# A gathered wide-and-deep network on one core: embedding rows and W1 kept on chip, waits and tail rearranged

## The reference

```python
emb = jax.vmap(lambda tab, idx: tab[idx])(tables, cat_features)      # 26 x 512 x 128
emb_btd = jnp.transpose(emb, (1, 0, 2))
wide_num = jax.nn.relu(numerical @ w_wide + b_wide)
linear_output = jnp.sum(emb_btd, axis=1) + wide_num                  # 512 x 128
x = jnp.concatenate([numerical, emb_btd.reshape(512, 26 * 128)], axis=1)
x = jax.nn.relu(x @ W1 + b1)                                         # W1: 3341 x 256
x = jax.nn.relu(x @ W2 + b2)                                         # 256 x 128
return jax.nn.sigmoid(x @ W3 + b3 + linear_output)                   # 512 x 128
```

## Time and profile before

| | |
|---|---|
| median of 3 runs | 145.16 us (144.66 to 145.37) |
| profiled execution, its own time | 145.52 us |
| its span | 143.7 us |
| PE busy, PEld busy | 89.8 us (62%), 46.8 us (33%) |
| DVE, ACT busy | 28.8 us (20%), 20.5 us (14%) |
| POOL busy | 99.2 us (69%) |
| mean granted TensorE clock | 0.877 of full |
| transfers | 10.75 MB, 75 GB/s over the span |

### The profile page before, as it was taken

One profiled execution on the slowest core, in us unless ns is written; L12 is line 12 of the kernel. 1 busy time (PEld: TensorE's weight loads), 2 busy tenths in 40 slices (PEclk: granted clock), 3 DMA queues, 4 the chain that ended last, 5 costly groups with the idle time before them and its releaser, 6 DMA issues.

```text
span 143.7 us, 1247 instructions
## 1 busy us (share of the span) xinstructions
PE 89.8 (62%) x278; PEld 46.8 (33%) x278; DVE 28.8 (20%) x78; ACT 20.5 (14%) x42; POOL 99.2 (69%) x111
## 2 busy tenths in 40 slices
PE   0588298609760793655944925916909809986891
PEld 0326234204320440232513404404404305444780
DVE  1402012203120211221211211302203202122461
ACT  0401011101110110110111101101101101122342
POOL 2677777777777777777777776776777777777400
PEclk9999999996899559995698797796895995999998
DMA  4424553571357347865254283393362481332311
GB/s 96 132 55 51 52 51 100 74 97 48 91 88 83 55 65 87 79 90 92 51 96 89 39 89 92 47 81 110 51 93 76 72 110 55 81 83 55 54 45 37
DMA packets 8901, 10.75 MB, mean 75 GB/s; under 512 B 3018, under 2 KB 7235, under 8 KB 8899
## 3 DMA queue, kind: packets, MB, share of 16 engines
q0 software_dynamic: 3328, 6.82, 36.6%
q1 hardware_dynamic: 4448, 3.67, 8.9%
q10 hardware_dynamic: 1123, 0.23, 0.8%
HBM read 10.45 MB, written 0.26 MB: 75 GB/s over the span
## 4 chain that ended last, share of the span: by engine, by line
DMA 39%; PE 27%; POOL 18%; issue 8%; POOLq 1%; DVE 0%; ACT 0%
DMA emb<-in_L_rec_tables,staged 35%; PE first_layer L232 15%; POOL emb L180 14%; PE turn L225 10%; POOL emb_tail L180 4%; DMA emb_tail<-in_L_rec_tables,row_idx 2%; DMA emb<-in_L_rec_tables,row_idx 2%; POOLq L31 1%; PE first_layer L283 1%; PE mlp L295 1%; PE scalars L305 0%; ACT y L484 0%; DVE h L417 0%; PE turn L273 0%; POOLq L198 0%
## 5 line engine op out<-in xcount | busy, mean ns | idle before, releaser
L180 POOL DMA_INDIRECT emb<-in_L_rec_tables,staged x88 | 83.0, 943 | 27.9 <-issue 22.6
L232 PE MATMUL first_layer<-emb_t,w 128*128 128x512 f32 x96 | 59.4, 753 | 0.4 <-DMA w<-in_L_rec_W 0.4
L225 PE MATMUL turn<-ident,emb 128*128 128x128 f32 x96 | 20.3, 350 | 42.9 <-DMA emb<-in_L_rec_tables,staged 38.8
L225 PEld LDWEIGHTS turn<-ident,emb 128*128 128x128 f32 x96 | 14.1, 176 | 64.7 <-DMA emb<-in_L_rec_tables,staged 56.1
L463 ACT COPY emb_t<-turn 128x512 f32<-128x512 f32 x24 | 14.0, 585 | 107.6 <-PE turn L225 107.6
L232 PEld LDWEIGHTS first_layer<-emb_t,w 128*128 128x128 f32 x96 | 21.5, 248 | 18.0 <-issue 16.9
L377 DVE TENSOR_TENSOR emb_sum<-turn,emb_sum 128x512 f32<-128x512 f32 x23 | 15.9, 692 | 39.2 <-ACT emb_t L463 39.2
L365 DVE COPY staged<-row_idx 128x4 int32 (+1 forms) x22 | 4.5, 209 | 55.5 <-DMA emb<-in_L_rec_tables,staged 55.4
L180 POOL DMA_INDIRECT emb_tail<-in_L_rec_tables,row_idx x8 | 7.5, 944 | 2.4 <-issue 2.4
L180 POOL DMA_INDIRECT emb<-in_L_rec_tables,row_idx x7 | 6.6, 943 | 2.1 <-issue 1.8
L283 PE MATMUL first_layer<-emb_tail_t,w_tail 128*128 128x128 f32 x32 | 4.9, 282 | 0.0
(11 more groups left out here) (37 smaller groups left out, 22.5 us busy)
## 6 DMA issues: line engine op xcount, KB each, us to landing
w<-in_L_rec_W SPq DMA_DIRECT2D x24, 128.0 KB, 3.0
emb<-in_L_rec_tables,staged POOLq DMA_INDIRECT x88, 3.6
w_tail<-in_L_rec_W SPq DMA_DIRECT2D x1, 256.0 KB, 3.2
out<-y SPq DMA_DIRECT2D x4, 64.0 KB, 1.8
w<-in_L_rec_W ACTq DMA_DIRECT2D x1, 128.0 KB
emb_tail<-in_L_rec_tables,row_idx POOLq DMA_INDIRECT x8, 2.9
emb<-in_L_rec_tables,row_idx POOLq DMA_INDIRECT x7, 3.8
cat_sb<-in_r_cat_features ACTq DMA_DIRECT2D x1, 52.0 KB
```

What stands on the lines that cost most here:

```text
L180: nc.gpsimd.indirect_dma_start(tile, None, rows, bass.IndirectOffsetOnAxis(ap=index, axis=0)).then_inc(landed, 16)
L225: mm = nc.tensor.transpose(turn[par][:, chunk(c)], emb[:, par, c, :], ident[:, :])
L232: mm = nc.tensor.matmul(first_layer[k][:, :], w1[:, par, chunk(k)], emb_t[:, par, :], start=False, stop=False, skip_group_check=True)
```

## The change

- All 26 tables' rows and all of W1 have a place of their own on chip. W1 comes in four loads at the start (tables 0-1, 2-7, 8-16, 17-25), and the body's loops are written out.
- POOL waits, before table t's gathers, for the landing of table t - 2 (AHEAD), with a semaphore for each table. `staged` and its copies are gone. The row offsets are added in one instruction for all 104 columns; wrap and clamp are done in another order (clamp to -V..V-1, then wrap), with as many instructions.
- TensorE does a table's first layer right behind ACT's copy of that table. `emb_t` has four slots, `turn` two.
- The wide part and the vectors stand ahead of table 0 in TensorE's list, in banks of their own.
- In the tail, `turn_sum` is a matmul of the chunk's `emb_sum` with the identity into a bank `final`, and layer 3 is added in the same bank, as a matmul of `h2` with W3 spread over 128 columns (`w3_wide`, made once by DVE). The sigmoid takes this bank, with the wide part as its bias; `add_wide` is gone. TensorE's order in the tail is another one (below). DVE still adds each tile behind ACT's copy.

The core of the diff (of `...` stretches, those with names alone and with lines removed are left out):

```diff
-PAIR = 2
+LATE = 2
+SLOTS = 4
+AHEAD = 2
+W1_CUTS = [0, 2, 8, 17, 26]
...
-        staged = sb("staged", [P, PAIR, CH], I32)
-        w1 = sb("w1", [P, PAIR, H1])
-        w1_tail = sb("w1_tail", [P, PAIR, H1])
+        w1 = sb("w1", [P, T, H1])
+        ones = sb("ones", [P, D])
+        w3_wide = sb("w3_wide", [P, D])
-        emb = sb("emb", [P, PAIR, CH, D])
-        emb_t = sb("emb_t", [P, PAIR, B])
-        emb_tail = sb("emb_tail", [P, CH, PAIR, D])
-        emb_tail_t = sb("emb_tail_t", [P, CH, PAIR, P])
+        emb = sb("emb", [P, T, CH, D])
+        emb_t = sb("emb_t", [P, SLOTS, B])
+        late_t = sb("late_t", [P, TILES, P])
-        logit = sb("logit", [P, CH])
...
-            def load_w1(step, par, first=False):
-                if not first:
-                    sp.wait_ge(used[par], step)
-                sp.dma_start(w1[:, par, :], W1[bass.ds(NUM + (step * PAIR + par) * D, D), :]
-                             ).then_inc(w1_loaded[par], 16)
-
-            for par in range(PAIR):
-                load_w1(0, par, first=True)
-            sp.dma_start(w1_tail[:, :, :], W1[NUM + TAIL * PAIR * D:NUM + T * D, :].rearrange("(g d) n -> d g n", d=D)
-                         ).then_inc(w1_tail_loaded, 16)
-            with sp.Fori(1, TAIL) as step:
-                for par in range(PAIR):
-                    load_w1(step, par)
+            for i, loaded in enumerate(w1_loaded):
+                lo, hi = W1_CUTS[i], W1_CUTS[i + 1]
+                sp.dma_start(w1[:, lo:hi, :], W1[NUM + lo * D:NUM + hi * D, :].rearrange("(t d) n -> d t n", d=D)
+                             ).then_inc(loaded, 16)
...
             gp.wait_ge(first_steps, 3)
-            gather(emb[:, 0, 0, :], first_row[:, :], gathered[0])
-            gp.wait_ge(first_rows_ready, 1)
-            for par in range(PAIR):
+            gather(0, 0, first_row[:, :], gathered[0])
+            gp.wait_ge(rows_ready, 1)
+            for t in range(BODY):
+                if t > AHEAD:
+                    gp.wait_ge(gathered[t - AHEAD], WHOLE)
                 for c in range(CH):
-                    if par + c == 0:
-                        continue
-                    gather(emb[:, par, c, :], column(par, c), gathered[par])
-            with gp.Fori(1, TAIL) as step:
-                for par in range(PAIR):
-                    gp.wait_ge(staged_ready[par], step)
-                    gp.wait_ge(turned[par], step)
-                    gp.sem_inc(slot_free, 1)
-                    for c in range(CH):
-                        gather(emb[:, par, c, :], staged[:, par, c:c + 1], gathered[par])
-            gp.wait_ge(rows_ready, 1)
-            for c in range(CH):
-                for g in range(PAIR):
-                    gather(emb_tail[:, c, g, :], column(TAIL * PAIR + g, c), tail_gathered[c * PAIR + g])
+                    if t + c > 0:
+                        gather(t, c, column(t, c), gathered[t])
+            gp.wait_ge(gathered[BODY - AHEAD], WHOLE)
+            for c in range(CH):
+                if c == CH // 2:
+                    gp.wait_ge(gathered[BODY - AHEAD + 1], WHOLE)
+                for g in range(LATE):
+                    gather(BODY + g, c, column(BODY + g, c), late_gathered[c * LATE + g])
...
+            pe.wait_ge(small_loaded, 16 * SMALL)
+            for c in range(CH):
+                mm = nc.tensor.matmul(wide_bank[:, c:c + 1], num_t[:, chunk(c)], w_wide_sb[:, :],
+                                      start=True, stop=True)
+            mm.then_inc(wide_done, 1)
+            nc.tensor.transpose(vec_bank[:, 0:KH + 2], vec_rows[:, :],
+                                ident[0:KH + 2, 0:KH + 2]).then_inc(vecs_turned, 1)
+
+            def turn_table(t):
+                pe.wait_ge(gathered[t], WHOLE)
+                if t >= 2:
+                    pe.wait_ge(added, t - 1)
                 for c in range(CH):
+                    mm = nc.tensor.transpose(turn[t % 2][:, chunk(c)], emb[:, t, c, :], ident[:, :])
+                mm.then_inc(turned, 1)
+
+            def sum_table(t):
+                if t in W1_CUTS:
+                    pe.wait_ge(w1_loaded[W1_CUTS.index(t)], 16)
+                pe.wait_ge(copied, t + 1)
+                for k in range(KH):
+                    mm = nc.tensor.matmul(first_layer[k][:, :], w1[:, t, chunk(k)], emb_t[:, t % SLOTS, :],
+                                          start=False, stop=False, skip_group_check=True)
+                mm.then_inc(used, 1)
+
+            for t in range(BODY):
+                turn_table(t)
+                sum_table(t)
+
+            def turn_tile(n):
+                c, g = divmod(n, LATE)
+                pe.wait_ge(late_gathered[n], 16)
+                if n < 2:
+                    pe.wait_ge(added, BODY - 1 + n)
                 else:
+                    pe.wait_ge(late_added, n - 1)
+                nc.tensor.transpose(turn[n % 2][:, 0:P], emb[:, BODY + g, c, :], ident[:, :]
+                                    ).then_inc(late_turned, 1)
+
+            def sum_tile(n):
+                c, g = divmod(n, LATE)
+                pe.wait_ge(late_copied, n + 1)
                 for k, (done, ready) in enumerate([(h1_low_done, h1_low_ready), (h1_high_done, h1_high_ready)]):
                     if c >= 1 and g == 0:
                         pe.wait_ge(ready, c)
+                    mm = nc.tensor.matmul(first_layer[k][:, chunk(c)], w1[:, BODY + g, chunk(k)], late_t[:, n, :],
+                                          start=False, stop=False, skip_group_check=True)
+                    if g == LATE - 1:
                         mm.then_inc(done, 1)
 
+            def turn_sum(c):
+                pe.wait_ge(late_added, (c + 1) * LATE)
+                if c == 0:
+                    pe.wait_ge(wide_ready, 1)
+                    pe.wait_ge(vecs_ready, 1)
                 if c >= 2:
                     pe.wait_ge(y_ready, c - 1)
+                nc.tensor.matmul(final[c % 2][:, 0:D], emb_sum[:, chunk(c)], ident[:, :],
+                                 start=True, stop=False, skip_group_check=True)
+
+            def layer2(c):
                 for k, ready in enumerate([h1_low_ready, h1_high_ready]):
                     pe.wait_ge(ready, c + 1)
                     mm = nc.tensor.matmul(mlp[c % 2][:, 0:P], w2[:, k, :], h1[:, k, chunk(c)],
...
             def layer3(c):
                 pe.wait_ge(h2_ready, c + 1)
                 if c == 0:
+                    pe.wait_ge(w3_ready, 1)
+                nc.tensor.matmul(final[c % 2][:, 0:D], h2[:, chunk(c)], w3_wide[:, :],
+                                 start=False, stop=True, skip_group_check=True).then_inc(final_done, 1)
+
+            for c in range(CH):
+                n = c * LATE
+                turn_tile(n)
+                if c >= 1:
+                    layer2(c - 1)
+                sum_tile(n)
+                if c >= 1:
+                    turn_sum(c - 1)
+                turn_tile(n + 1)
+                if c >= 1:
+                    layer3(c - 1)
+                sum_tile(n + 1)
+            turn_sum(CH - 1)
+            layer2(CH - 1)
             layer3(CH - 1)
...
+            nc.vector.memset(ones[:, :], 1.0).then_inc(ones_ready, 1)
...
+            nc.vector.tensor_tensor(row_idx[:, :], idx_bank[:, 0:T * CH], base[:, :, :].rearrange("p t c -> p (t c)"),
+                                    ALU.add).then_inc(rows_ready, 1)
...
+            nc.vector.tensor_scalar(w3_wide[:, :], ones[:, :], w3_col, None, ALU.mult).then_inc(w3_ready, 1)
+
+            for t in range(BODY):
+                dve.wait_ge(copied, t + 1)
+                if t == 0:
+                    nc.vector.tensor_copy(emb_sum[:, :], turn[0][:, :]).then_inc(added, 1)
+                else:
+                    dve.wait_ge(added, t)
+                    nc.vector.tensor_tensor(emb_sum[:, :], turn[t % 2][:, :], emb_sum[:, :], ALU.add
+                                            ).then_inc(added, 1)
...
+            def add_tile(n):
+                c = n // LATE
+                dve.wait_ge(late_copied, n + 1)
+                if n == 0:
+                    dve.wait_ge(added, BODY)
+                elif n % LATE > 0:
+                    dve.wait_ge(late_added, n)
+                nc.vector.tensor_tensor(emb_sum[:, chunk(c)], turn[n % 2][:, 0:P], emb_sum[:, chunk(c)], ALU.add
+                                        ).then_inc(late_added, 1)
+
+            for c in range(CH):
+                n = c * LATE
                 if c >= 1:
                     relu_h1_high(c - 1)
+                add_tile(n)
+                if c >= 1:
+                    relu_h2(c - 1)
+                add_tile(n + 1)
             relu_h1_high(CH - 1)
             relu_h2(CH - 1)
...
+            for t in range(BODY):
+                act.wait_ge(turned, t + 1)
+                if t >= SLOTS:
+                    act.wait_ge(used, t - SLOTS + 1)
+                nc.scalar.copy(emb_t[:, t % SLOTS, :], turn[t % 2][:, :]).then_inc(copied, 1)
+
```

(15 more changed lines are left out.)

249 lines of the change are left out of this document (50 added, 199 removed).

## The result

| | before | changed |
|---|---|---|
| median beside each other | 145.27 us (144.66 to 146.06, 18 runs) | 145.78 us (145.27 to 147.75, 18 runs) |
| ratio | | 1.0049, 95% interval 1.0026 to 1.0073 |
| the same kernel on a later occasion (e18_alone) | 145.13 us (17 runs) | 145.79 us (12 runs), ratio 1.0059 (1.0021 to 1.0096) |
| profiled execution, its own time and span | 145.52 / 143.7 us | 147.32 / 145.5 us |

The changed kernel is half a per cent slower; 144.6 was forecast. Its times fall into two groups: of the 30 executions of both occasions 11 lie at 146.79 to 147.75, and all others but one (146.14) at 145.27 to 145.87. The trace of the first occasion is one of the upper group, that of e18_alone (145.87) one of the lower.

What follows compares the result with a forecast made beforehand. POOL's gathers, then the dependent work after the last one, bound the kernel. POOL's -1.09 less 1.28 lost at tile 7, with a shorter tail, gave -0.51: 145.0 profiled, less 0.36 for the median, 144.6 us; range 143.3 to 146.7.

Steps and rivals of the forecast that it cites:

- POOL, -1.09: POOL's four stalls ahead of tables that reuse a slot go, since it waits for landings, not transposes: -1.09 us.
- D: Rival: W1's burst reaches POOL at the wait ahead of table 3 or the indices' landing; 145.1 to 146.1, chance 0.10.
- Where the gain is lost: Tile stage at the end: table 23's 3 us are never caught up, tile 7 turns 1.28 us after landing.
- From one layer 2 to the next: TensorE's tile stage: one chunk's cycle takes 2.58 us, while two tiles are gathered in 2.50.
- From there: Tail from tile 7's turn to the end of the last sigmoid: 3.33 us in place of 3.98.
- The store: The store behind the last sigmoid stays at 2.4 us.
- From the profiled execution to the median, -0.36: Last step: the median lies 0.36 us under the profiled execution, taking 145.0 to 144.6.
- Rival B: TensorE meets the end at half clock at table 23's transposes and sums: +2.2 us, 146.8 in full; chance 0.28.
- The sum's bank: Chunk end: without add_wide and chunk 2's transpose and layer 2 ahead of chunk 3's, the tail takes 3.33 for 3.98.

Runs made afterwards that it cites:

- e18_alone: The changed kernel itself, unchanged, with only the kernel before beside it; 145.79 us, ratio 1.0059 to the kernel before.
- e6_turned: e3_both with POOL waiting again for the transposes of the table two before instead of its landing; 146.22 us, ratio 1.0061 to the kernel before.
- e2_tail: The changed kernel with the old order of the tile stage on TensorE, DVE and ACT, body as changed; 144.44 us, ratio 0.9934 to the kernel before.
- e3_both: The changed kernel with both old orders, in the body and in the tile stage; 144.44 us, ratio 0.9933 to the kernel before.
- e5_warm20: The changed kernel with three dummy matmuls of 512 columns behind table 20's first layer; 145.38 us, ratio 1.0020 to the kernel before.
- e1_body: The changed kernel with the old body order, a table's sum behind the next table's transposes, tile stage as changed; 145.64 us, ratio 1.0013.
- e7_wide: e3_both with the old chunk end: transposed sum in layer 2's bank, layer 3 with one column, add_wide on DVE; 144.14 us, ratio 0.9916.
- e8_order: e3_both with the tile stage's lists for TensorE, DVE and ACT written out in an order found by search; 144.17 us, ratio 0.9930.

## Why the prediction was wrong

- **POOL, -1.09: right in size, its cause not shown.** Its last gather is at 132.78 and 132.60 (forecast 132.90), with no stall. The prediction gave all four stalls to the wait for transposes and put the loop and the staged copies at 0. e6_turned has the old wait in a written-out list and none of the four, so what goes away with the loop may be all of the 0.99. That no landing reaches the wait (D) held, although W1's burst did reach TensorE: the wide part waited for its load until 11.95 and table 0 was turned at 14.18, where it was turned at 10.65 before. The prediction took two or three us; it was 3.5. In e6_turned the same lateness cost POOL 2.6 us, so the new wait earns its place at the start, by a term that the sum did not have. Table 1's rows landed there by 17.95, 5.2 after its last gather at 12.77, some 1 us ahead of the wait for them, which the changed kernel reaches near 18.9. Behind this stands the Trainium skill, "DMA: Bandwidth & Descriptors", section "Queues, rings and completion order", with its turns between queues: the trace agrees, since the gathers beside the burst landed, in the changed kernel the first of them in 6.8 us and none in more.
- **Where the gain is lost: right in kind.** Table 23 stands 3 us ahead of a stage that never catches up, as the prediction said with 1.28 lost; e2_tail and e3_both confirm that it is this order's: there TensorE waits for tiles 3 and 5.
- **The failed step: "From one layer 2 to the next", 2.58 us, and "From there", 3.33.** They measured 2.79 and 3.63. Both steps took every instruction at the length that it has in a row without a wait, 0.61 for four. In the new order the first group behind each hand-over takes 0.10 more, by the rows above for a weight load that nothing hides: by the starts in e18_alone 0.11 at layer 2 (134.44 to 134.99, taken as 0.44) and 0.09 at the odd tile's sum (0.52 from its start at 136.29 to ACT's relu, taken as 0.43), 0.20 of the cycle's 0.21. In the tail it comes three times. Against the 140.81 of the forecast e5_warm20 has -0.10 up to chunk 0's layer 2, +0.43 for two cycles, +0.12 up to tile 7's turn and +0.29 from there: 141.55. The row of before at 125.01, shown above, had the 0.10 in it.
- **The store: 2.4 taken, 1.9 measured.** From the last sigmoid to the end of the execution 3.78 in place of 4.20: -0.42. This is luck: the prediction kept the store without a look at how close the last sigmoids stand, and the error hid more than half of the 0.74 above.
- **From the profiled execution to the median, -0.36: wrong.** The kernel before scatters (144.66 to 146.06) and its profiled execution was in the upper half. e5_warm20's profiled execution, 145.33, is its median within 0.05. Taking that off was worth 0.36 in the wrong direction.
- **Rival B: right in price, a little off in place, its share too small.** It was forecast at 0.28, +2.2, for a half clock at table 23. The clock fell ahead of table 21, in the trace of the kernel before (the transposes at 118.44 above, then a sum of 3.24) as in both of the changed one and in those of e1_body, e2_tail, e3_both, e6_turned, e7_wide and e8_order; e5_warm20's stayed up. Lasting one table it cost the changed kernel 0.54 (e18_alone against e5_warm20), lasting two 2.02; 11 of 30 executions lie where the second would put them. No median hangs on it alone: it moves it from 145.33 to 145.78, by 0.45. In the kernel before and in the old tile stage TensorE caught up after the same fall: it still waits for transfers ahead of its last tiles.
- **The sum.** Together 144.65 + 0.74 - 0.42 + 0.36 = 145.33, the level of e5_warm20, and with the half clock 145.78. The measured time lies inside the range (143.3 to 146.7), the direction was wrong: an error of 1.1 us made of three of 0.32, 0.36 and 0.45, all to the same side.
- **The sum's bank, taken as 3.33 in place of 3.98 in the tail:** e7_wide ends 0.29 earlier with the old chunk end. Its tail from tile 7's turn is as long as that of before (3.99), and in the same order the new form takes 4.23, so there it saves nothing. The 3.33, measured 3.63, comes from the new order, which has chunk 2 done before tile 7.

## What to carry to other kernels

Price a matmul group by whether it stands behind a wait: here the first after each hand-over cost 0.10 us more, with its weight load in the open, and an order that puts each product right behind its own copy pays that at every step. Keep another tile's work between a copy and its use where the engine is the chain, and shorten a producer's list only together with a look at whether the consumer still waits for it. A change of several parts is to be priced and run part by part: here the rows and W1 on chip with the new wait and the written-out loops made 1.2 us, and the two new orders and the sum's bank together took some 1.7 back. A stall priced by its engine's own timeline is to be set beside the end of what it waited for: the distance, 0.80 here, shows how much of it is the wait and how much the engine's own loop.
